# Attention probabilities split while still in PSUM, with half of each transpose moved to the DMA engines

## The chip, the cores and the metric

The kernel runs on one core of a Trainium2 chip. The metric is device time in microseconds (us) of one execution; lower is better. The core has five engines with programs of their own: TensorE (PE: matmuls and transposes, operands from SBUF, results to PSUM), VectorE (DVE), ScalarE (ACT), GpSimd (POOL, which here touches SBUF only) and SyncE (SP, which issues DMAs). Each runs its program strictly in order, and they meet at semaphores.

## The reference, cut to what matters

The input x is 4 sequences of 512 tokens of width 256, float32. It is layer-normalised, goes through attention, and independently through a mixture-of-experts layer; the output is x + attention * silu(experts).

```
xn = layernorm(x)
q, k, v = xn @ Wq, xn @ Wk, xn @ Wv          # 16 query heads, 4 key/value heads, head width 128
q, k = rotary embedding and positional scaling of q and k
scores = q k^T / sqrt(128), causal mask        # 512 x 512 for each of 4 x 16 heads
attn = softmax(scores)                         # exp(s - max) / sum
s = (attn @ v) @ Wo
g = silu(top-2-of-16 routed experts(xn) + shared experts(xn))
out = x + s * g
```

All matrix products are to be of nearly float32 precision. The kernel has no float32 matmul in its large products. It splits every operand into a 16-bit high half (float16) and a 16-bit low half (bfloat16, the rest after the high half is subtracted) and makes three passes: high*high, high*low, low*high.

## The kernel before, in words

The attention is done in 16 rounds (`NG`), one for each pair of batch and key/value head; a round has 4 query heads, 64 in all. Rounds 0, 1 and 2 ("first", "second", "third") also carry the transposes of the normalised x, the router and the placing of tokens with experts. Rounds 3 to 13 are a hardware loop over one body, round 14 runs the same body, and round 15 ("last") has no projections of queries and keys for a next round. Then come the expert steps: 40 tile steps of the shared experts and 48 tiles of the routed ones.

The order of the work on every engine is written out by hand in a `round_` function for each engine. All are built of stages j = 0, 1, 2 and a tail. Stage j works on the scores of head j+1 while the probabilities of head j are transposed; the tail transposes head 3 and scores the next round's head 0. Spread over the stages are the projections of the next round's queries and key (`project`, with their rotary products in `rotate_products` on DVE, a sum on POOL, the high half on ACT, the low half on POOL), this round's values (`project_values`), and the output projection of the last round's heads (`project_out`, added up by `add_projection` on DVE).

A head's probabilities go this way:

1. PE `score` (L1380): three passes of four causal row blocks of 128 queries with 128, 256, 384 and 512 keys, into three PSUM banks (units 0, 1, 2: the block of 512; the blocks of 384 and 128; the block of 256). A unit may be overwritten when its exponentials are done (L1386).
2. DVE `row_max` (L1089): adds the mask, takes the negated maximum of a row. Four instructions with four short reads of the accumulator.
3. ACT `exponentials` (L771): exp(s - max) from PSUM into `probs` in SBUF, float32, with the row sum as a by-product.
4. DVE `invert_sums` (L1100): one reciprocal of the four sums. It stands inside `rotate_products`, after the first of its three products.
5. POOL `divide` (L535): multiplies the probabilities by the reciprocal, four instructions.
6. PE `transpose_probs` (L1395): ten float32 transposes of 128x128 into two PSUM banks, in three units (4, 4 and 2 blocks). Units 0 and 1 stand early in the stage, unit 2 late.
7. ACT `probs_hi` (L781) copies each unit to SBUF as float16; DVE `probs_lo` (L1104) subtracts that from the bank and writes bfloat16. These are the halves of the transposed probabilities `pT`.
8. PE `weigh_values` (L1408): three passes of four matmuls over `pT` and the values, for head j-1 in stage j; ACT `output_hi` and DVE `output_lo` split the result.

SP issues its DMAs in the order of its own program: the weights, the fill of a DRAM buffer for routed rows, then (after the last attention weight is split) the shared experts' weights, and the routed experts' weights through a ring of five slots. `load_rows` (L478) later issues DMA transposes of 128x512 two-byte values from that DRAM buffer, once for each routed tile.

Of the kernel before, what the change touches and what calls it, by code (L numbers as in the profile page):

```python
# [10 lines left out]
F32 = mybir.dt.float32  # L11
# [7 lines left out]
P = 128  # L19
# [47 lines left out]
PCOLS = 1280  # L67

# [116 lines left out]
def build(nc, x, wq, wk, wv, wo, gate_t, w_gate_up, w_down, shared_gu, shared_down, rope, ident, mask, iota, tri, rows, digits, lag_digits, out):  # L185
    with ExitStack() as ctx:
# [74 lines left out]
        ARENA = 102400  # L261
# [20 lines left out]
        probs = [carve(PCOLS, F32) for _ in range(2)]  # L282
        pT = [split(PCOLS) for _ in range(2)]
# [32 lines left out]
        score_bank, pt_bank, o_bank, misc_bank = bank[0:3], bank[3:5], bank[5], bank[6:8]  # L316
# [17 lines left out]
        scores, maxed, exped, inverted, normed = sem("scores"), sem("maxed"), sem("exped"), sem("inverted"), sem("normed")  # L334
        pt_ps, pt_hi, pt_lo = sem("pt_ps"), sem("pt_hi"), sem("pt_lo")
# [21 lines left out]
        W_FIRST = 4  # L357

# [52 lines left out]
        def _(sp):  # L411
# [31 lines left out]
            sp.wait_ge(filled, 1)  # L443
            xs_tiles = xs_dram.rearrange("(t p) d -> p t d", p=P)
            for c in range(FILLS):
                sp.dma_start(xs_tiles[:, c * FILL_TILES:(c + 1) * FILL_TILES], fill).then_inc(fill_out, 16)

# [14 lines left out]
            for e in range(E_ROUTED):  # L462
                if e == ERING - E_SHARED:
                    sp.wait_ge(shared_w, 2)
                if e >= ERING:
                    sp.wait_ge(expert_low, e - ERING + 1)
                at = e % ERING * WE
                sp.dma_start(stage[:, at:at + WG].rearrange("p (c n) -> p c n", c=KC),
                             w_gate_up[e].rearrange("(c p) n -> p c n", p=P)).then_inc(expert_in[e % ERING], 16)
                sp.dma_start(stage[0:HC, at + WG:at + WE].rearrange("p (c n) -> p c n", c=2),  # L470
                             w_down[e].rearrange("(c p) n -> p c n", p=HC)).then_inc(expert_in[e % ERING], 16)
                if e == E_ROUTED - 1:

                    sp.wait_ge(scattered, SCATTERED)
                    sp.dma_start(meta[:], xs_tiles[:, :, D:DX]).then_inc(meta_in, 16)
# [247 lines left out]
        def _(act):  # L723
# [110 lines left out]
            def round_(rd):  # L834
                for j in range(GH - 1):
# [4 lines left out]
                    if j == 2:  # L840
                        output_hi(rd, 0)
# [783 lines left out]
```

## Time and profile before

| | us |
|---|---|
| median of 3 executions | 738.01 |
| lowest, highest | 737.32, 740.93 |
| span of the profiled execution, first to last instruction | 735.7 |
| PE busy (matmuls) | 659.1 |
| DVE busy | 581.6 |
| POOL busy | 537.8 |
| ACT busy | 442.3 |

No time of the profiled execution as a whole stands beside its span; the median lies 2.3 us above the span. In the profile "busy" is the time in which an engine has at least one instruction under way. Instructions of one engine overlap a little, so the distance between the starts of two successive ones is often shorter than the duration of the first; where an engine's capacity is the question, the distance between starts counts. A bracket at the end of a row gives the time that the engine stood idle before it and what it waited for. In names of tiles, "arena" is the large SBUF buffer in which most attention and expert tiles lie, and "bank" is PSUM.

The part of the page that follows the chain of work which ended last shows, by engine, shares of the span of 41% for POOL, 19% for issue, 17% for PE, 13% for DVE and 7% for ACT.

### The profile page before, as it was taken

What the parts mean: (1) busy time and instruction counts of PE and PEld (TensorE: products, weight loads), DVE (VectorE), ACT (ScalarE), POOL (GpSimd) and SP (SyncE); (2) the same over time, 40 slices, a digit from 0 to 9 for tenths busy, and PEclk for the clock granted to TensorE, in tenths of its full rate; (3) what the DMA queues carried; (4) which work ended last, traced back from release to release, by engine and by line L of the source; (5) the groups of instructions that cost most, each with busy time, mean ns of one, the idle gap of its engine ahead of it and who ended that gap; (6) DMA issues with size and microseconds to landing.
All of it is one profiled execution on the core that took longest, in us unless ns stands there. A gap on an engine that the chain in (4) does not pass through costs nothing.

```text
span 735.7 us, 17233 instructions
## 1 busy us (share of the span) xinstructions
PE 659.1 (90%) x4994; PEld 460.8 (63%) x4995; DVE 581.6 (79%) x1683; ACT 442.3 (60%) x1205; POOL 537.8 (73%) x588
## 2 busy tenths in 40 slices
PE   3678869789999999999999999999987899999992
PEld 1255546556766667676666766667665577767761
DVE  6988879789999999998999999999876344333378
ACT  3585636465657666575675657668584664555542
POOL 4677777978888887888877888888988993555510
PEclk9899989999999999999999999999998999999996
DMA  9491000500000000000000000000122564665772
GB/s 306 165 301 48 1 0 2 141 22 16 0 14 14 0 14 0 14 7 7 14 0 14 0 14 14 0 14 2 35 70 88 167 117 105 138 141 138 210 285 101
DMA packets 64952, 50.44 MB, mean 69 GB/s; under 512 B 35252, under 2 KB 58260, under 8 KB 64916
## 3 DMA queue, kind: packets, MB, share of 16 engines
q1 hardware_dynamic: 60804, 39.45, 19.3%
q0 software_dynamic: 3840, 10.52, 4.3%
q8 instruction: 20, 0.33, 0.2%
q14 instruction: 16, 0.13, 0.1%
q10 hardware_dynamic: 272, 0.02, 0.0%
HBM read 24.72 MB, written 18.96 MB: 59 GB/s over the span
## 4 chain that ended last, share of the span: by engine, by line
POOL 41%; issue 19%; PE 17%; DVE 13%; ACT 7%; DMA 2%; POOLq 0%; SPq 0%; DVEq 0%
POOL arena L539 16%; PE bank L1546 8%; POOL arena L533 8%; POOL arena L526 7%; PE bank L1576 6%; POOL xs_dram L586 4%; ACT arena L777 3%; POOL compare L582 2%; PE bank L1555 2%; DVE arena L1108 2%; POOL arena L563 1%; ACT arena L785 1%; DVE arena L1082 1%; DVE arena L1083 1%; DVE arena L1078 1%
## 5 line engine op out<-in xcount | busy, mean ns | idle before, releaser
L539 POOL TENSOR_TENSOR arena<-arena,rinv 128x128 f32<-128x128 f32 (+3 forms) x256 | 176.4, 720 | 83.5 <-DVE rinv L1102 83.4
L777 ACT ACTIVATE arena<-bank,nmax 128x512 f32<-128x512 f32 (+3 forms) x256 | 132.5, 535 | 64.6 <-DVE nmax L1096 64.6
L1096 DVE CUSTOM_DVE_ANT_0 bank<-bank,mask_b 128x512 f32<-128x512 f32 (+3 forms) x256 | 118.1, 516 | 14.2 <-issue 14.2
L1390 PE MATMUL bank<-arena 128*128 128x512 f16 (+7 forms) x768 | 116.4, 302 | 5.9 <-POOL arena L533 5.9
L785 ACT CAST arena<-bank 128x512 f16<-128x512 f32 (+1 forms) x192 | 93.3, 522 | 45.1 <-PE bank L1403 43.5
L1359 PE MATMUL bank<-xnT_hi,arena 128*128 (+1 forms) x320 | 111.0, 389 | 9.2 <-DVE arena L1083 4.7
L1419 PE MATMUL bank<-arena 128*128 128x512 f16 (+7 forms) x768 | 118.0, 305 | 0.0
L1403 PE MATMUL bank<-ident_f,arena 128*128 128x128 f32 x640 | 93.5, 277 | 25.5 <-DVE arena L1108 14.5
L1108 DVE TENSOR_TENSOR arena<-bank,arena 128x512 bf16<-128x512 f32 (+1 forms) x192 | 109.0, 595 | 3.9 <-ACT arena L785 1.8
L526 POOL TENSOR_TENSOR arena<-arena 128x512 f32<-128x512 f32 x77 | 98.6, 1281 | 2.5 <-DVE arena L1083 2.2
L1403 PEld LDWEIGHTS bank<-ident_f,arena 128*128 128x128 f32 x640 | 74.0, 142 | 38.9 <-DVE arena L1108 18.3
L1390 PEld LDWEIGHTS bank<-arena 128*128 128x128 f16 (+1 forms) x768 | 66.2, 98 | 48.1 <-issue 7.9
L533 POOL TENSOR_TENSOR arena<-arena 128x512 bf16<-128x512 f32 x80 | 92.5, 1161 | 4.8 <-ACT arena L765 4.8
L1435 PE MATMUL bank<-arena 128*128 (+2 forms) x768 | 94.6, 274 | 1.6 <-DVE logit L1048 1.2
L1419 PEld LDWEIGHTS bank<-arena 128*128 128x128 f16 (+1 forms) x768 | 68.3, 99 | 38.3 <-issue 2.4
L1435 PEld LDWEIGHTS bank<-arena 128*128 (+2 forms) x768 | 75.3, 98 | 19.9 <-issue 1.7
L1283 DVE TENSOR_TENSOR arena<-bank,arena 128x176 f32<-128x176 f32 x80 | 27.2, 340 | 73.3 <-ACT arena L912 71.8
L718 POOL DMA_INDIRECT ys_dram<-arena,row_u x48 | 46.0, 959 | 51.2 <-ACT arena L923 51.2
L765 ACT CAST arena<-arena 128x512 f16<-128x512 f32 x80 | 50.3, 629 | 53.9 <-POOL arena L526 49.3
L1359 PE MATMUL bank<-xnT_lo,arena 128*128 (+1 forms) x160 | 61.9, 387 | 0.0
L1359 PEld LDWEIGHTS bank<-xnT_hi,arena 128*128 (+1 forms) x320 | 31.9, 100 | 45.5 <-issue 8.3
L1082 DVE TENSOR_TENSOR arena<-bank,tab 64x512 f32<-64x512 f32 x80 | 55.4, 693 | 2.2
(147 smaller groups left out, 1158.9 us busy)
## 6 DMA issues: line engine op xcount, KB each, us to landing
xs_dram<-s_sb SPq DMA_DIRECT2D x4, 1548.0 KB, 14.4
stage<-w_gate_up SPq DMA_DIRECT2D x16, 352.0 KB
arena<-ys_dram SPq DMA_DIRECT2D x8, 512.0 KB, 6.5
stage<-w_down SPq DMA_DIRECT2D x16, 176.0 KB
stage<-wq SPq DMA_DIRECT2D x4, 512.0 KB, 8.0
stage<-wo SPq DMA_DIRECT2D x4, 512.0 KB, 6.5
stage<-x SPq DMA_DIRECT2D x1, 2048.0 KB, 10.6
out<-s_sb SPq DMA_DIRECT2D x8, 256.0 KB, 2.1
```

The lines of the kernel that those rows point to most:

```text
L526: pool.tensor_tensor(rot_a[buf], rot_a[buf], rot_b[buf], ALU.add).then_inc(rot_add, 1)
L533: pool.tensor_tensor(dst, rot_a[buf], hi, ALU.subtract).then_inc(rot_lo, 1)
L539: ins = pool.tensor_tensor(pr, pr, rinv[:, par, qt:qt + 1].to_broadcast([P, (qt + 1) * P]), ALU.mult)
L777: ins = act.activation(probs[par][:, P_AT[qt]:P_AT[qt] + n], score_bank[u][:, col:col + n], ACT.Exp, scale=-1.0, bias=nmax[:, par, qt:qt + ...
L785: act.copy(pT[j % 2][0][:, at:at + cols], pt_bank[(3 * j + u) % 2][:, 0:cols]).then_inc(pt_hi, 1)
L1096: ins = dve.tensor_tensor_reduce(score_bank[u][:, col:col + n], score_bank[u][:, col:col + n], mask_b[:, S - n:S], -1.0, 3e38, ALU.add, AL ...
L1108: dve.tensor_tensor(pT[j % 2][1][:, at:at + cols], pt_bank[(3 * j + u) % 2][:, 0:cols], pT[j % 2][0][:, at:at + cols], ALU.subtract).then_ ...
L1359: ins = pe.matmul(ps[:], w[a][:, c * chunk:c * chunk + DH], tokens[m][:, c * TOK:c * TOK + S], start=(c == 0 and n == 0), stop=(c == KC - ...
L1390: ins = pe.matmul(score_bank[u][:, col:col + n_k], qT[a][:, j * S + qt * P:j * S + (qt + 1) * P], kT[m][:, 0:n_k], start=(n == 0), stop=(n ...
L1403: ins = pe.transpose(pt_bank[(3 * j + u) % 2][:, col + (qt - kt) * P:col + (qt - kt + 1) * P], probs[j % 2][:, P_AT[qt] + kt * P:P_AT[qt] ...
L1419: ins = pe.matmul(o_bank[:, kt * P:S], v_s[a][:, kt * DH:(kt + 1) * DH], pT[j % 2][m][:, PT_AT[kt]:PT_AT[kt] + n_q], start=(kt == 0 and n ...
L1435: ins = pe.matmul(ps[:, 0:D], heads[a][:, j * S + q * P:j * S + (q + 1) * P], w[m][:, j * D:(j + 1) * D], start=(j == 0 and n == 0), stop= ...
```

## The change

- PSUM: the scores get four banks in place of three, used in turn (`score_at`: unit 3j+u modulo 4). The transposed probabilities get one bank, read as 2048 bytes of bfloat16 a partition, in place of two.
- ACT `exponentials` writes the exponentials back into the score bank in place.
- DVE `invert_sums` stands directly after `row_max`, and not within the rotary products.
- POOL `divide` is gone.
- ACT `probs_hi` now reads the exponentials in PSUM, multiplies by the reciprocal and writes the float16 high half `p_hi` of the untransposed probabilities: four instructions a head.
- DVE `probs_lo` now computes exponential * reciprocal - `p_hi` from PSUM in one instruction for a row block and writes bfloat16 `p_lo`: four instructions a head, the first block inside the rotary products, the other three behind them. A score bank is free when this is done, so PE `score` waits for `p_lo_ready`, where it waited for `exped`.
- SP `transpose_hi` transposes `p_hi` by four DMA transposes a head (of 4, 3, 1 and 2 blocks of 128x128), SBUF to SBUF, into `pT_hi`. SP's program gets the same rounds as the other engines; the loads of the experts' weights are placed between them.
- PE `transpose_probs` transposes `p_lo` only, ten bfloat16 transposes against a bfloat16 identity, in two units (8 and 2 blocks). ACT `pT_lo_out` copies them to SBUF.
- PE `weigh_values` makes the two passes over the high halves first (waiting for the DMAs), then the pass over the low halves.
- In stage 2, DVE's `output_lo` of head 0 stands between `row_max` and `invert_sums`, where it stood before `row_max`. In the tail, `output_lo` of head 2 stands before `row_max`, where it stood behind it; ACT's `probs_hi` for the next round's head 0 stands behind `rotate_hi("q2")` and the second `pT_lo_out`.

The core of the diff:

```diff
-PT_UNITS = [[(0, 0)], [(1, 0), (3, 384)], [(2, 0)]]
+PT_UNITS = [[(0, 0), (1, 512), (3, 896)], [(2, 0)]]
-PT_UNIT_COLS = [(0, 512), (512, 512), (1024, 256)]
+PT_UNIT_COLS = [(0, 1024), (1024, 256)]
+SCORE_BANKS = 4
...
-        probs = [carve(PCOLS, F32) for _ in range(2)]
-        pT = [split(PCOLS) for _ in range(2)]
+        p_hi = [carve(PCOLS, F16) for _ in range(2)]
+        p_lo = [carve(PCOLS, BF16) for _ in range(2)]
+        pT_hi = [carve(HI_COLS, F16) for _ in range(2)]
+        pT_lo = [carve(PCOLS, BF16) for _ in range(2)]
...
+            def transpose_hi(rd, j):
+                h, par = rd.head(j), j % 2
+                if not (isinstance(h, int) and h < 2):
+                    sp.wait_ge(pv, h - 1)
+                for u, unit in enumerate(SCORE_UNITS):
+                    sp.wait_ge(p_hi_ready, h * 3 + u + 1)
+                    sp.sem_inc(hi_seen)
+                    for qt, _ in unit:
...
+                        sp.dma_start_transpose(dst, p_hi[par][:, P_AT[qt]:P_AT[qt] + n].bitcast(BF16)).then_inc(pT_hi_in[par], 16)
...
-            def divide(h, par):
-                pool.wait_ge(inverted, h + 1)
-                for qt in range(QT):
...
                     for qt, col in SCORE_UNITS[u]:
+                        p = score_at(j, u)[:, col:col + (qt + 1) * P]
+                        ins = act.activation(p, p, ACT.Exp, scale=-1.0, bias=nmax[:, j % 2, qt:qt + 1], accum_out=rsum[:, j % 2, qt:qt + 1])
...
+            def probs_hi(rd, j):
+                h, par = rd.head(j), j % 2
+                act.wait_ge(inverted, h + 1)
+                if not (isinstance(h, int) and h < 2):
+                    act.wait_ge(pT_hi_in[par], hi_landed(rd, j - 2))
+                for u, unit in enumerate(SCORE_UNITS):
                     for qt, col in unit:
                         n = (qt + 1) * P
+                        ins = act.activation(p_hi[par][:, P_AT[qt]:P_AT[qt] + n], score_at(j, u)[:, col:col + n], ACT.Copy,
+                                             scale=rinv[:, par, qt:qt + 1])
+                    ins.then_inc(p_hi_ready, 1)
+
+            def pT_lo_out(h, j, units):
                 for u in units:
                     at, cols = PT_UNIT_COLS[u]
+                    act.wait_ge(pt_ps, h * 2 + u + 1)
+                    act.copy(pT_lo[j % 2][:, at:at + cols], pt_bank[:, 0:cols]).then_inc(pt_lo, 1)
...
                     if j == 2:
                         output_hi(rd, 0)
+                    exponentials(h, j + 1)
+                    pT_lo_out(rd.head(j), j, (0,))
+                    probs_hi(rd, j + 1)
...
                 dve.tensor_tensor(rot_a[buf], ps[:], tab[:, cos, :], ALU.mult)
                 half = DH // 2
-                if inverted_head is not None:
-                    invert_sums(*inverted_head)
+                if lows is not None:
+                    probs_lo(*lows, (0,))
...
             def probs_lo(h, j, units):
+                par = j % 2
                 for u in units:
+                    if u == 0 and not (isinstance(h, int) and h < 2):
+                        dve.wait_ge(pt_ps, h * 2 - 2)
+                    dve.wait_ge(p_hi_ready, h * 3 + u + 1)
+                    for qt, col in SCORE_UNITS[u]:
+                        n, at = (qt + 1) * P, P_AT[qt]
+                        ins = dve.scalar_tensor_tensor(p_lo[par][:, at:at + n], score_at(j, u)[:, col:col + n], rinv[:, par, qt:qt + 1],
+                                                       p_hi[par][:, at:at + n], ALU.mult, ALU.subtract)
+                    ins.then_inc(p_lo_ready, 1)
...
                 for j in range(GH - 1):
                     h, par = rd.head(j + 1), (j + 1) % 2
+                    row_max(h, j + 1)
                     if j == 2:
                         output_lo(rd, 0)
-                    row_max(h, par)
+                    if rd.first and j == 0:
+                        first_rope("q3", PROLOGUE.rot("q1"))
+                    invert_sums(h, par)
+                    if rd.first:
+                        x_items_lo(rd, X_BEFORE[j])
+                    rope(("q0", "q1", "k")[j], (h, j + 1))
...
-                probs_lo(rd.head(3), 3, (0, 1))
+                output_lo(rd, 2)
                 if not rd.last:
-                    row_max(rd.head(GH), 0)
-                output_lo(rd, 2)
+                    row_max(rd.head(GH), GH)
...
-                    if reuse:
-                        pe.wait_ge(exped, h * 3 + u - 2)
+                    if not (isinstance(h, int) and h * 3 + u < SCORE_BANKS):
+                        pe.wait_ge(p_lo_ready, h * 3 + u - (SCORE_BANKS - 1))
...
                     if u == 0:
-                        pe.wait_ge(normed, h + 1)
+                        pe.wait_ge(p_lo_ready, h * 3 + 3)
...
+                pe.wait_ge(pT_hi_in[j % 2], hi_landed(rd, j))
+                for a in range(2):
+                    for kt in range(QT):
+                        pe.matmul(o_bank[:, kt * P:S], v_s[a][:, kt * DH:(kt + 1) * DH], pT_hi[j % 2][:, hi_at(kt):hi_at(kt) + (QT - kt) * P],
+                                  start=(a == 0 and kt == 0), stop=False)
+                pe.wait_ge(pt_lo, h * 2 + 2)
+                for kt in range(QT):
+                    ins = pe.matmul(o_bank[:, kt * P:S], v_s[0][:, kt * DH:(kt + 1) * DH], pT_lo[j % 2][:, PT_AT[kt]:PT_AT[kt] + (QT - kt) * P],
+                                    start=False, stop=(kt == QT - 1))
```

## Rows read from the trace of the kernel before

**Rows 1.** Windows: length, busy PE, PEld, DVE, ACT, POOL; clock, DMA share, GB/s.

```profile
85.00:120.00 35.00, 27.67 (x190) 18.34 (x191) 27.06 (x80) 17.00 (x49) 23.71 (x28) 0.90 0.00 1
200.00:520.00 320.00, 314.99 (x2417) 219.98 (x2415) 294.85 (x856) 206.61 (x583) 264.27 (x296) 1.00 0.02 9
```

**Rows 2.** Waits, 200 to 520 us: who for whom; us, times, longest.

```profile
POOL arena L539 <- DVE rinv L1102: 50.4, 29, 3.1
...
DVE bank L1096 <- issue: 7.8, 10, 0.8
```

**Rows 3.** Page's costliest groups, POOL's divisions: busy us, mean ns; idle before.

```profile
L539 POOL TENSOR_TENSOR arena<-arena,rinv 128x128 f32<-128x128 f32 (+3 forms) x256 | 176.4, 720 | 83.5 <-DVE rinv L1102 83.4
```

**Rows 4.** Timeline of PE in the loop: start us, us, instructions.

```profile
302.46 1.47 PE L1435 MATMUL bank<-arena 128*128 x12
303.77 1.04 PE L1403 MATMUL bank<-ident_f,arena 128*128 128x128 f32 x8
304.65 1.79 PE L1419 MATMUL bank<-arena 128*128 128x512 f16 x12
306.60 1.80 PE L1390 MATMUL bank<-arena 128*128 128x512 f16 x12 [0.16 <-POOL arena L533]
308.24 0.38 PE L1359 MATMUL bank<-xnT_hi,arena 128*128 x1
308.45 0.38 PE L1359 MATMUL bank<-xnT_lo,arena 128*128 x1
...
317.50 0.28 PE L1374 MATMUL bank<-arena,xnT_hi 128*128 x2
```

**Rows 5.** Groups by form, 200 to 520 us: busy us, mean ns; idle.

```profile
L1108 DVE TENSOR_TENSOR arena<-bank,arena 128x512 bf16<-128x512 f32 x82 | 52.7, 684 | 1.3
...
L1108 DVE TENSOR_TENSOR arena<-bank,arena 128x256 bf16<-128x256 f32 x41 | 17.1, 417 | 0.3
...
L785 ACT CAST arena<-bank 128x512 f16<-128x512 f32 x82 | 44.0, 590 | 24.0 <-PE bank L1403 24.0
...
L777 ACT ACTIVATE arena<-bank,nmax 128x512 f32<-128x512 f32 x41 | 28.5, 695 | 34.6 <-DVE nmax L1096 34.6
```

**Rows 6.** Timeline of DVE: one head's row maxima and reciprocal.

```profile
312.84 0.69 DVE L1096 CUSTOM_DVE_ANT_0 bank<-bank,mask_b 128x512 f32<-128x512 f32 x1
...
314.61 0.14 DVE L1096 DVE_READ_ACCUMULATOR2_ANT nmax<- 128x1 f32 x1
...
315.90 0.18 DVE L1102 RECIPROCAL rinv<-rsum 128x4 f32<-128x4 f32 x1 [0.52 <-ACT arena L777]
```

**Rows 7.** Timeline of ACT: the same head's exponentials and casts behind.

```profile
313.63 0.69 ACT L777 ACTIVATE arena<-bank,nmax 128x512 f32<-128x512 f32 x1 [2.35 <-DVE nmax L1096]
...
315.75 1.08 ACT L785 CAST arena<-bank 128x512 f16<-128x512 f32 x2
316.70 0.65 ACT L765 CAST arena<-arena 128x512 f16<-128x512 f32 x1
```

**Rows 8.** Timeline of DVE: reciprocals around the early rounds, and the last one.

```profile
32.78 0.17 DVE L1102 RECIPROCAL rinv<-rsum 128x4 f32<-128x4 f32 x1
...
150.50 0.17 DVE L1102 RECIPROCAL rinv<-rsum 128x4 f32<-128x4 f32 x1
...
551.32 0.18 DVE L1102 RECIPROCAL rinv<-rsum 128x4 f32<-128x4 f32 x1 [1.25 <-ACT arena L777]
```

**Rows 9.** DMA transposes by source line; queue 1 from 600 to 680 us.

```profile
L480 SPq DMA_TRANSPOSE arena<-xs_dram x48: 1188/1193/4862, 593.6 to 689.1; - x48
...
DMA to landing us min/median/max: 2.6/3.3/4.8
...
q1 hardware_dynamic: 21927, 5.29, 36.4%
```

**Rows 10.** Timeline of PE in the last round.

```profile
555.36 0.66 PE L1403 MATMUL bank<-ident_f,arena 128*128 128x128 f32 x4 [2.33 <-POOL arena L539]
...
559.23 3.41 PE L1419 MATMUL bank<-arena 128*128 128x512 f16 x12
```

More of the change, by code:

```diff
@@ L459, in _ @@
             sp.dma_start(stage[0:SHARED_ROWS[-1], at + full * D:at + (full + 1) * D], shared_down[full * P:, :]).then_inc(shared_in, 16)
[L462 to L475, printed above, removed]
+            for e in range(ERING - E_SHARED):
+                load_expert(e)
+            with sp.Fori(3, NG - 2) as i:
+                round_(Round(i, "loop"))
+            round_(Round(NG - 2, "loop"))
+            sp.wait_ge(shared_w, 2)
+            for e in range(ERING - E_SHARED, ERING):
+                load_expert(e)
+            round_(Round(NG - 1, "last"))
+            for e in range(ERING + 1, E_ROUTED):
+                sp.wait_ge(expert_low, e - ERING + 1)
+                load_expert(e)
+            sp.wait_ge(scattered, SCATTERED)
+            sp.dma_start(meta[:], xs_tiles[:, :, D:DX]).then_inc(meta_in, 16)
             def load_rows(m, k):
@@ L808, in _ @@
             exponentials(0, 0, (1, 2))
+            probs_hi(Round(0, "first"), 0)
             normalise(1)
@@ L841, in round_ @@
                         output_hi(rd, 0)
+                    exponentials(h, j + 1)
+                    pT_lo_out(rd.head(j), j, (0,))
+                    probs_hi(rd, j + 1)
                     if j == 0:
-                        if rd.first:
-                            probs_hi(rd.head(j), j, (0, 1))
-                        exponentials(h, par)
-                        if not rd.first:
-                            probs_hi(rd.head(j), j, (0, 1))
                         rotate_hi("q3", rd.i * 5 + 5)
@@ L859, in round_ @@
                     else:
-                        probs_hi(rd.head(j), j, (0, 1))
-                        exponentials(h, par)
                         if rd.first:
@@ L881, in round_ @@
                     rotate_hi("k", rd.rot("k"))
-                probs_hi(rd.head(3), 3, (0, 1))
+                pT_lo_out(rd.head(3), 3, (0,))
                 output_hi(rd, 2)
@@ L887, in round_ @@
                 else:
-                    exponentials(rd.head(GH), 0)
+                    exponentials(rd.head(GH), GH)
                     rotate_hi("q2", rd.rot("q2"))
-                probs_hi(rd.head(3), 3, (2,))
+                pT_lo_out(rd.head(3), 3, (1,))
+                if not rd.last:
+                    probs_hi(rd, GH)
             round_(Round(0, "first"))
@@ L1193, in round_ @@
                             tile_experts(0)
-                    probs_lo(rd.head(j), j, (2,))
                     if rd.first:
@@ L1217, in round_ @@
                     tile_experts(1)
-                rope("q3", None if rd.last else (rd.head(GH), 0))
-                probs_lo(rd.head(3), 3, (2,))
+                if not rd.last:
+                    invert_sums(rd.head(GH), 0)
+                rope("q3", None if rd.last else (rd.head(GH), GH))
                 if rd.first:
```

150 lines of the change are left out of this document (78 added, 72 removed).

## The prediction

> **What bounds the kernel now.** I read the table of busy time by stretch first. From 200 to 520 us, nearly all of it the loop body, TensorE is busy 315.0 of 320 us and VectorE 294.9 [rows 1]. From 150.50 to 551.32 us lie 51 heads [rows 8], so a head takes 7.86 us and a round of four 31.4 us. TensorE is the bound; VectorE at 92% stands idle only 2.5 us a round. The waits say the same: the longest is GpSimd's wait for the reciprocal, 50.4 us, of an engine with time to spare, while VectorE's largest is 7.8 us in ten rounds, for scores [rows 2]. The page's chain gives GpSimd 41%, but each of its pieces is released by the other engines in turn, and TensorE is full; I do not read it as a GpSimd bound. The order of the steps then decides. The thing to see in the kernel before: the first rotary product, and in two stages of three also a head's two `probs_lo`, lie on VectorE between `row_max` and the reciprocal, so that the exponentials finish behind useful work.
>
> **TensorE.** The change halves the transposes. Eight float32 blocks take from 303.77 to 304.65, 0.11 us each; a 16-bit matmul of the same 128 columns adds about 0.06 (0.28 for two, of which one alone lasts some 0.22) [rows 4]. Ten a head: 0.55 us less, 2.2 us a round. The rest of TensorE's work is unchanged. Its need falls from 0.984 of 31.4 = 30.9 to 28.7 us a round.
>
> **GpSimd.** Four divisions go, 176.4 us in all, 2.75 a head [rows 3]. It is not the bound, so this pays only where others wait for it: in the early rounds.
>
> **ScalarE.** Out: casts of 1280 columns a head (590 ns for 512 [rows 5]; two in a row and the start of the next come 0.95 us apart [rows 7]), about 1.35 us. In: the same number of columns out of the bfloat16 bank, as one of 1024 and one of 256. No row shows a 1024-column cast from PSUM; twice the two casts' 0.475 is 0.95, and one instruction of that length saves one fixed part at most, so 0.85 to 0.95; I take 0.94. Also in: four scaled copies, no row; the exponentials, of the same shapes and with a pointer operand, are nearest (695 ns for 512 [rows 5]), the plain cast's 590 is the lower end. I take 0.69 us for the first and about 1.7 us of the engine for all. ScalarE's load goes from 206.6/320 of a round, 20.3 us, to about 26.5. It is no bound, but it stands in a chain.
>
> **VectorE.** Out: three subtractions, 684 + 684 + 417 ns [rows 5]. In: four instructions of 512, 384, 256 and 128 columns. By the slope between 684 and 417, 1.04 ns a column, they are 684 + 551 + 417 + 284 = 1936 ns, 0.15 us more a head, 0.6 a round. `scalar_tensor_tensor` is in no row; bounds -0.1 us a head (the four overlap at their edges) and +0.4 us (0.1 an instruction for the pointer operand, the excess of 695 over 590 on the other engine). Busy time a round: 0.921 x 31.4 = 28.9, plus 0.6 = 29.5 us. That is already above TensorE's 28.7: VectorE becomes the engine with the most work, and every wait in its program now lengthens the round. The new order makes three.
>
> *First wait: for the exponentials.* `invert_sums` stands right behind `row_max`. The last read of the maxima ends at 314.61 + 0.14 = 314.75; the exponentials end so that the reciprocal starts at 315.90 [rows 6], 1.15 us later, although they began at 313.63, right after the first maximum [rows 7]. In the last round the same wait shows at 1.25 us where nothing covers it [rows 8]. Before, the first product covered 0.6 of it or all. Now nothing does, but in stage 2 `output_lo` (about 0.6 us) lies in it. Per round 4 x 1.13 - 0.6 = 3.9 us.
>
> *Second wait: for the high half.* ScalarE, done with the exponentials, first copies 1024 transposed columns of the head before (0.94), then makes the high half of the first block (0.69), 1.63 us in all. VectorE meanwhile does the reciprocal (0.18) and the first product (0.69), and ScalarE's 1.63 began 0.1 before. 0.65 us remain a head, 2.7 a round (in the tail a rotary cast and a 256-column copy stand in place of the 1024-column copy, about as long). Bounds: 0.3 with the lower prices above, 1.1 if ScalarE is late for the transposes.
>
> *Third wait: in the tail.* `output_lo` of head 2 moved ahead of `row_max`. It needs, after VectorE's last low half but one: the bank that `add_projection` frees (0.8), `project_out` (1.31 us, 302.46 to 303.77), eight transposes (0.44), `weigh_values` (1.79) [rows 4], and `output_hi` on ScalarE (0.59, a cast like those of rows 5): 4.9 us. VectorE has 3.65 us of work there (0.35 + 0.35 + 0.6 + 2.0 + 0.35). 1.2 us a round; bounds 0 and 2.
>
> Sum of a loop round: 29.5 + 3.9 + 2.7 + 1.2 = 37.3 us, against 31.4: +5.9. Rounds 3 to 14 are twelve: +71. TensorE, 28.7 of 37.3 us, then has slack in each stage; the scores' new wait for `p_lo` costs it 0.3 us a head (the last unit), which falls into that slack.
>
> **Early rounds.** From the first reciprocal to the thirteenth the three take 117.7 us [rows 8]. From 85 to 120 us VectorE is busy only 27.1 of 35 [rows 1], partly waiting for the router's steps on GpSimd, which get 2.75 us a head of room. The same three waits would add 17.7; I give back 10: +8. **Last round and after.** No rotary products there; the end loses GpSimd's division between the last reciprocal and the last transposes (TensorE waits 2.33 us for it [rows 10]), gains ScalarE's and VectorE's steps: -2, bounds -4 and +3. The expert steps and their loads are unchanged. Total: +77.
>
> The profiled span is 735.7, the median 738.0, 2.3 above it. 735.7 + 77 + 2.3 = **815 us**.
>
> **DMA transposes.** Four DMAs a head go to SP's queue, 256 in all. In the expert steps a transpose of four blocks holds SP 1.19 us and lands 3.3 us after issue; queue 1 carried forty of them from 600 to 680 us at 36.4% of all engines, 0.73 us each [rows 9]. Ten blocks a head are 1.8 us of the DMA engines and at most 4.8 us of SP, inside 9.3 us. The high half is made about one and a half stages, 14 us, before `weigh_values` needs it, and the last of four issued in a row would land at about 8 us. So hidden; but these rows read DRAM, and none has SBUF as source. If the four run strictly one after another at 3.3 us, a head takes 13.2 us: a rival.
>
> **A rule that speaks for the change.** No row here has ScalarE writing to PSUM. The Trainium skill, "ScalarE: Activation LUTs", section on what happens when an `exp` ACTIVATE runs, says that ScalarE's writes to PSUM are faster than those to SBUF. By it the first wait would be shorter. No trace here can show it yet, and ScalarE still has to work off four instructions of which only the first overlaps the maxima, so it moves my sum by no more than the bounds below.
>
> **Rivals.**
> - *Only the first wait counts.* The scaled copies and the wide cast come out short, and the tail's chain is ready: 29.1 + 3.9 = 33.0 a round, +1.6 x 12 = 19, early +2, end -2: 757 us. For it: the two other waits are differences of small sums. Against: the 1024-column copy stands in the program between exponentials and high half, whatever its price. 14%.
> - *TensorE's clock falls in the gaps.* From 200 to 520 us it was granted in full (1.00, 2.4 GHz), from 85 to 120, with long gaps, 0.90 [rows 1]. After a gap of 2.33 us and another like it, twelve matmuls took 3.41 us in place of 1.79, its lower level of 1.2 GHz [rows 10, 4]. TensorE will now be idle 8 to 9 us a round, in pieces up to 2 us. At half clock the tail's chain is up to 3.5 us longer, and the score before each `row_max` 0.3 a head: +4.5 a round more, about 54: 869 us. The Trainium skill, "TensorE: Matmul & The Clock Gate", Part 1, says that activity releases the throttle and idle time brings it back; by that rule, which rows 10 agree with, this rival is live. Against it: between the gaps stand 5 to 7 us of dense work. 7%.
> - *Transposes from SBUF run one after another*, as above: ScalarE's `probs_hi` waits for the transposes two heads back and all follows: 64 x 13.2 = 845 in place of 519 (the 64 heads from 32.78 to 551.32): about 1060 us. 4%.
> - *Faster: TensorE stays the bound.* The mechanism: the exponentials, written to PSUM, end right behind the maxima, the high half follows at once, and TensorE keeps its order with 2.2 us less of transposes a round. It decides where VectorE's waits in sum fall below 31.4 - 29.5 = 1.9 us a round. Without any wait the round is 29.5, -1.9 x 12 = -23, early rounds -5, end -2: 708 us. Against it is the 1.15 us between the last maximum and the reciprocal, 3.9 a round, by itself too much. 6%.
> - *No change*, the same with waits of just that size: 2%.
>
> **How the numbers follow.** Forecast 67%, of its own 785 to 845 us; the rest as above. The range, 755 to 860, takes in the first rival and leaves out the clock's full price, the serial transposes and the faster side. Within 0.5% is about what a measurement of this kernel can tell from no change: 734 to 742. Slower 0.91, same 0.03, faster 0.06.
>
> **What would show it.** In the profile after: VectorE's idle time before `invert_sums` about 1.1 us a head, put down to ScalarE; idle before the first `probs_lo` about 0.65; idle before one `output_lo` a round about 1.2; a round of about 37 us; TensorE busy about 77% in the loop at a clock of 1.00; transposes on TensorE at half their spacing; DMA share near 0.2; no wait of TensorE or ScalarE on DMAs. It would be wrong if VectorE's low halves cost well below 0.5 us a block, if ScalarE's writes to PSUM shortened the exponentials by much, or if the DMA transposes held `weigh_values` up.

## The result and the profile after

The changed kernel takes 857.05 us (median of 4 runs, 856.83 to 857.18) where the kernel before takes 737.86: a ratio of 1.1605, interval 1.158 to 1.1631. Slower was forecast, and 857 lies inside the range of 755 to 860, 3 us below its upper end; the predicted 815 is 42 us too low.

The profiled execution took 857.14 us, its span 855.2. First the page of the kernel after: the busy times, the chain that ended last by engine, and three of its costliest groups (busy us, mean ns of one | idle of the engine before it, and for whom).

```profile
PE 659.4 (77%) x4930; PEld 428.3 (50%) x4995; DVE 605.0 (71%) x1747; ACT 544.7 (64%) x1397; POOL 365.2 (43%) x332
...
DVE 28%; PE 23%; ACT 21%; issue 20%; POOL 3%; DMA 2%; DVEq 1%; ACTq 1%; SPq 0%
...
L1167 DVE SCALAR_TENSOR_TENSOR arena<-bank,rinv,arena 128x512 bf16<-128x512 f32 (+3 forms) x256 | 128.8, 546 | 48.7 <-ACT arena L831 46.7
L839 ACT COPY arena<-bank 128x1024 bf16<-128x1024 bf16 (+1 forms) x128 | 91.9, 718 | 30.9 <-PE bank L1463 30.9
L1463 PE MATMUL bank<-ident_b,arena 128*128 128x128 bf16 x640 | 60.8, 229 | 54.1 <-ACT arena L839 54.0
```

No engine is full any more. The chain, 41% GpSimd before, is now shared about equally by VectorE, TensorE and ScalarE: work handed from one to the next and back. The next table is of the loop body of the kernel after, with the columns of [rows 1]:

```profile
250.00:600.00 350.00, 272.39 (x2059) 170.89 (x2092) 271.16 (x782) 235.29 (x616) 130.76 (x113) 0.97 0.17 40
```

TensorE is busy 78% of the stretch where it was 98% [rows 1], GpSimd 37%, and the DMA share is 0.17. The reciprocals of the heads mark the time, as in [rows 8]. In the kernel after it runs at 31.89 us (first head), 173.87 (thirteenth), 650.77 (61st) and 675.52 (last); before, at 32.78, 150.50, 531.44 and 551.32. So the 119.5 us of added span are:

- early rounds (three): 117.7 to 142.0 us, +24.3
- the twelve rounds between the thirteenth and the 61st: 31.75 to 39.74 us each, +96
- last round: 19.9 to 24.8 us, +4.9
- what lies ahead, -0.9; from the last reciprocal to the end (184.4 to 179.7), -4.7.

Where a round of another kernel is given below, it is the mean of the same twelve, read in the same way.

Where a loop round loses them is seen in the waits of the kernel after, 250 to 600 us (who for whom: us, times, longest), 8.8 rounds:

```profile
PE bank L1450 <- DVE arena L1167: 41.8, 34, 1.8
DVE rinv L1156 <- ACT bank L819: 36.9, 36, 1.2
DVE arena L1167 <- ACT arena L831: 25.8, 36, 1.4
PE bank L1463 <- ACT arena L839: 23.6, 18, 1.8
...
DVE arena L1174 <- ACT arena L853: 13.9, 9, 1.5
```

The three lines that begin with DVE are the three forecast waits, in the forecast places: 4.2, 2.9 and 1.6 us a round. With 30.8 us of work (271.16 of 350, of 39.74 us) they make 39.5 of the 39.74 us. TensorE's largest wait is for the low halves themselves, and its next for ScalarE's copy out of the transposes' bank: it follows VectorE and ScalarE. Its busy time, 30.9 us a round (272.39 of 350, of 39.74 us), is as large as VectorE's 30.8, so the busy times alone would not tell which of the two holds the round. Two stretches of VectorE's timeline show them at their instructions (the wait stands in brackets):

```profile
388.80 0.14 DVE L1150 DVE_READ_ACCUMULATOR2_ANT nmax<- 128x1 f32 x1
...
390.09 0.18 DVE L1156 RECIPROCAL rinv<-rsum 128x4 f32<-128x4 f32 x1 [1.16 <-ACT bank L819]
390.28 0.69 DVE L1131 TENSOR_TENSOR arena<-bank,tab 128x512 f32<-128x512 f32 x1
391.66 0.75 DVE L1167 SCALAR_TENSOR_TENSOR arena<-bank,rinv,arena 128x512 bf16<-128x512 f32 x1 [0.69 <-ACT arena L831]
...
408.41 0.69 DVE L1174 TENSOR_TENSOR arena<-bank,arena 128x512 f32 x1 [1.54 <-ACT arena L853]
```

What ScalarE did meanwhile, in its own timeline:

```profile
389.95 1.01 ACT L839 COPY arena<-bank 128x1024 bf16<-128x1024 bf16 x1
390.84 1.81 ACT L831 ACTIVATE arena<-bank,rinv 128x512 f16<-128x512 f32 x4
```

It copies the transposed columns of the head before first, and only then makes the high half that VectorE stands waiting for.

### The profile page after: what moved, and what is told of

Read it like the earlier page. It is cut to its first block, busy times and chain, and to the rows that moved or that the text cites. A ratio compares the mean times of both kernels' runs of the same rounds, so it can differ in the third digit from the quotient of the medians.

```text
span 855.2 us, 18017 instructions
## 1 busy us (share of the span) xinstructions
PE 659.4 (77%) x4930; PEld 428.3 (50%) x4995; DVE 605.0 (71%) x1747; ACT 544.7 (64%) x1397; POOL 365.2 (43%) x332
## 4 chain that ended last, share of the span: by engine, by line
DVE 28%; PE 23%; ACT 21%; issue 20%; POOL 3%; DMA 2%; DVEq 1%; ACTq 1%; SPq 0%
DVE arena L1167 11%; ACT bank L819 10%; PE bank L1608 7%; ACT arena L831 6%; PE bank L1638 5%; DVE arena L1136 3%; DVE arena L1135 3%; ACT arena L839 3%; PE bank L1497 2%; PE bank L1418 2%; PE bank L1477 2%; POOL arena L608 2%; DVE arena L1174 1%; PE bank L1617 1%; PE bank L1463 1%
## 5 line engine op out<-in xcount | busy, mean ns | idle before, releaser
L819 ACT ACTIVATE bank<-bank,nmax 128x512 f32<-128x512 f32 (+3 forms) x256 | 127.7, 500 | 142.3 <-DVE nmax L1150 142.3
L1450 PE MATMUL bank<-arena 128*128 128x384 f16 (+2 forms) x763 | 130.0, 307 | 75.4 <-DVE arena L1167 72.5
L1167 DVE SCALAR_TENSOR_TENSOR arena<-bank,rinv,arena 128x512 bf16<-128x512 f32 (+3 forms) x256 | 128.8, 546 | 48.7 <-ACT arena L831 46.7
L1450 PEld LDWEIGHTS bank<-arena 128*128 128x128 f16 (+1 forms) x768 | 64.3, 99 | 127.5 <-DVE arena L1167 91.1
L831 ACT ACTIVATE arena<-bank,rinv 128x512 f16<-128x512 f32 (+3 forms) x256 | 115.7, 556 | 0.5 <-DVE rinv L1156 0.5
L839 ACT COPY arena<-bank 128x1024 bf16<-128x1024 bf16 (+1 forms) x128 | 91.9, 718 | 30.9 <-PE bank L1463 30.9
L1463 PE MATMUL bank<-ident_b,arena 128*128 128x128 bf16 x640 | 60.8, 229 | 54.1 <-ACT arena L839 54.0
L1477 PE MATMUL bank<-arena 128*128 128x512 f16 (+3 forms) x512 | 88.1, 319 | 1.5 <-DVE arena L1174 1.5
L1463 PEld LDWEIGHTS bank<-ident_b,arena 128*128 128x128 bf16 x640 | 44.2, 103 | 79.7 <-ACT arena L839 62.2
L1477 PEld LDWEIGHTS bank<-arena 128*128 128x128 f16 (+1 forms) x512 | 47.3, 104 | 31.5 <-issue 7.1
L1174 DVE TENSOR_TENSOR arena<-bank,arena 128x512 f32 (+1 forms) x64 | 43.9, 685 | 26.8 <-ACT arena L853 26.7
```

What stands on the lines that cost most here:

```text
L819: ins = act.activation(p, p, ACT.Exp, scale=-1.0, bias=nmax[:, j % 2, qt:qt + 1], accum_out=rsum[:, j % 2, qt:qt + 1])
L831: ins = act.activation(p_hi[par][:, P_AT[qt]:P_AT[qt] + n], score_at(j, u)[:, col:col + n], ACT.Copy, scale=rinv[:, par, qt:qt + 1])
L839: act.copy(pT_lo[j % 2][:, at:at + cols], pt_bank[:, 0:cols]).then_inc(pt_lo, 1)
L1167: ins = dve.scalar_tensor_tensor(p_lo[par][:, at:at + n], score_at(j, u)[:, col:col + n], rinv[:, par, qt:qt + 1], p_hi[par][:, at:at + n] ...
L1450: ins = pe.matmul(score_at(j, u)[:, col:col + n_k], qT[a][:, j % GH * S + qt * P:j % GH * S + (qt + 1) * P], kT[m][:, 0:n_k], start=(n == ...
L1463: ins = pe.transpose(pt_bank[:, col + (qt - kt) * P:col + (qt - kt + 1) * P], p_lo[j % 2][:, P_AT[qt] + kt * P:P_AT[qt] + (kt + 1) * P], i ...
```

## The experiments

Twelve kernels: eight from the kernel after, four from the kernel before. Times are medians of the runs, ratios are to the kernel before (739.8 to 741.7 us in these batches).

### The order of two steps on ScalarE

```
                     exponentials(h, j + 1)
-                    pT_lo_out(rd.head(j), j, (0,))
                     probs_hi(rd, j + 1)
+                    pT_lo_out(rd.head(j), j, (0,))
```

> Changed kernel (857 us, loop round 40.2 us); in stages 0 to 2 ScalarE makes the high half of the new head before it copies the 1024 transposed low-half columns of the head before. Theory (VectorE is a chain of waits in program order): the second wait, 0.7 + 0.7 + 1.0 us a round before the first probs_lo, goes; 2.4 x 15 = 36 us, about 821 us, and the idle time before probs_lo is near zero in three stages. Rival (TensorE's one bank for transposes takes over): the copy is 1.8 us later, the second transposes and weigh_values behind it wait that much longer, the next scores come late and VectorE waits for them in place of the high half: 845 us or more.

Measured: 911.35 us, ratio 1.2292 (1.2214 to 1.2369); a round 43.96 us. Waits and stretch, 250 to 570 us:

```profile
PE bank L1463 <- ACT arena L839: 48.2, 20, 3.7
...
DVE bank L1150 <- issue: 24.7, 14, 3.1
...
250.00:570.00 320.00, 246.78 (x1706) 153.15 (x1734) 223.80 (x633) 192.51 (x494) 108.06 (x93) 0.88 0.15 36
```

The high half comes at once, and the copy comes late: both transposed units of a head share one bank, so TensorE waits for the copy (48.2 us in 7.3 rounds, against 23.6 in 8.8), the next scores come late, and VectorE waits for those instead. The rival (845 us or more) held, and the time went well beyond it. In this stretch TensorE's granted clock is 0.88 where it was 0.97; how much of the loss is the clock's and how much the late copy's is not separated. The second wait cannot be had back by turning these two steps round.

### The reciprocal and the low halves behind the rotary products

The reciprocal goes behind the first product and all low halves behind the whole rotary item, so that both waits have work in front of them (in round 0 the reciprocal stays where it was).

```
-                if lows is not None:
-                    probs_lo(*lows, (0,))
+                if lows is not None and inv:
+                    invert_sums(lows[0], lows[1] % 2)
...
-                        probs_lo(*lows, (1, 2))
+                        probs_lo(*lows, (0, 1, 2))
...
-                    invert_sums(h, par)
+                    if rd.first:
+                        invert_sums(h, par)
```

> Changed kernel; on VectorE the reciprocal stands again behind the first rotary product, and all three products stand before the head's low halves (in round 0 the reciprocal stays where it is). Theory: the exponentials are covered by 0.6 us of work and the high half by 1.4 us more: the first wait falls from 1.16 to 0.5 in three stages and to about 0 in one, the second to 0: 2.4 + 2.4 us a round, 15 rounds, about 785 us. Rival (TensorE or ScalarE sets the round, VectorE's waits are only where it shows): the waits move behind row_max or to output_lo, and the time stays above 840 us.

Measured: 784.68 us, ratio 1.0594 (1.0559 to 1.0629); a round 34.46 us. Timeline of VectorE, and the stretch 250 to 570 us:

```profile
409.76 0.18 DVE L1156 RECIPROCAL rinv<-rsum 128x4 f32<-128x4 f32 x1 [0.61 <-ACT bank L819]
...
411.39 1.93 DVE L1167 SCALAR_TENSOR_TENSOR arena<-bank,rinv,arena 128x512 bf16<-128x512 f32 x4
...
250.00:570.00 320.00, 276.72 (x2189) 178.74 (x2228) 282.00 (x830) 248.78 (x654) 145.24 (x124) 1.00 0.20 47
```

No instruction was added or taken away, and 72 us are back, as expected (about 785). The low halves start without a wait, the reciprocal waits less than half as long (17.4 us in 9.3 rounds against 36.9 in 8.8). VectorE is at 88% of the stretch; in the kernel before it was at 92% [rows 1].

### The DMA transposes left out

```
+                        continue
                         sp.dma_start_transpose(dst, p_hi[par]...)
...
-                pe.wait_ge(pT_hi_in[j % 2], hi_landed(rd, j))
```

> Changed kernel without the 256 DMA transposes and without the waits for them; weigh_values reads a high half that is zeroed once, so the attention output lacks its high part. Theory (the transposes are hidden): 857 us within 4 us. Rival (they hold up weigh_values, or their traffic slows the engines' SBUF accesses): 850 us or less.

Measured: 859.72 us, ratio 1.1617 (1.1583 to 1.1651), interval overlapping that of the kernel after. The DMA share falls from 0.17 to 0.02 (same columns as above) and nothing else moves:

```profile
250.00:600.00 350.00, 272.50 (x2065) 171.09 (x2099) 270.28 (x781) 233.95 (x613) 132.07 (x114) 0.97 0.02 7
```

The transposes from SBUF are hidden whole.

### The tail's order

```
-                output_lo(rd, 2)
                 if not rd.last:
                     row_max(rd.head(GH), GH)
+                output_lo(rd, 2)
```

> Changed kernel; in the tail VectorE's output_lo of head 2 stands behind row_max again, as in the kernel before. Theory A (the third wait, 1.5 us a round, is a wait for a chain that the scores need too, since score follows weigh_values on TensorE): VectorE then waits for the scores instead, and only the 0.6 us of output_lo that now lie in the wait for the exponentials are won: 0.6 x 15 = 9 us, about 848 us. Theory B (as my prediction put it, the wait is output_lo's own): 2.1 us a round, about 826 us.

Measured: 845.47 us, ratio 1.1432 (1.1401 to 1.1462); a round 38.77 us, 0.97 less. The wait of 1.54 us is gone, and VectorE waits ahead of the maxima instead, which leaves the reciprocal behind them a wait of 0.61:

```profile
402.93 0.69 DVE L1150 CUSTOM_DVE_ANT_0 bank<-bank,mask_b 128x512 f32<-128x512 f32 x1 [1.34 <-issue]
...
406.00 0.18 DVE L1156 RECIPROCAL rinv<-rsum 128x4 f32<-128x4 f32 x1 [0.61 <-ACT bank L819]
```

So the tail's wait costs 1 us a round net: its place is taken by the scores. This is theory A; theory B, the prediction's view that the wait is `output_lo`'s own, is out.

### TensorE kept busy in its gaps

```
+                    if warm and u > 0:
+                        for _ in range(8 - 2 * u):
+                            pe.matmul(o_bank[:], qT[0][:, 0:P], kT[0][:, 0:S], start=True, stop=True)
```

> Changed kernel; in stage 0 of each round but the first, TensorE runs 6 and 4 more matmuls of 512 columns into the bank that weigh_values overwrites next, in the two gaps (1.83 and 1.50 us) in which it waits for the low halves. Theory (the clock falls in these gaps, and the slower projection and transposes delay ScalarE's copy and with it VectorE's second wait in this stage, 1.0 to 1.4 us in place of 0.6): granted clock 1.00 in the loop, 0.4 to 0.8 us a round, 846 to 851 us. Rival (the clock costs nothing, all in slack): 857 us, or more by the added matmuls.

Measured: 858.34 us, ratio 1.1583 (1.1538 to 1.1628); a round 39.41 us.

```profile
250.00:570.00 320.00, 263.98 (x2011) 161.07 (x2009) 249.01 (x717) 215.71 (x566) 121.75 (x105) 1.00 0.17 39
...
DVE arena L1167 <- ACT arena L831: 21.2, 33, 0.7
```

The granted clock is back at 1.00. The second wait, by stage (tail, 0, 1, 2; means of the twelve rounds), goes from 0.57, 0.97, 0.69 and 0.69 us to 0.57, 0.65, 0.69 and 0.69: only that of stage 0, which has these gaps, gets shorter, and by as much as the round, 0.3 us. The added matmuls themselves delay nothing, for TensorE still waits for the low halves behind them:

```profile
412.38 0.83 PE L1455 MATMUL bank<-arena 128*128 128x384 f16 x6 [0.54 <-DVE arena L1167]
...
414.71 0.50 PE L1455 MATMUL bank<-arena 128*128 128x256 f16 x3 [0.64 <-DVE arena L1167]
```

So in the loop the fall of the clock to 0.97 costs 0.3 us of a round. The twelve rounds gain 4 us and the early ones 1, but from the 61st reciprocal to the end the profiled execution takes 3 us longer (204.5 to 207.7), and the time stays the same. The run adds nothing to round 0, where the granted clock is 0.83 with and without it.

### Reordering further

Three kernels on top of the reciprocal's move: with the reciprocal behind the second product and the tail order; with the reciprocal behind the first and the tail order; and with the low half's transposes in two banks, which takes one bank from the scores.

```
-SCORE_BANKS = 4
+SCORE_BANKS = 3
...
+        pt_bank = [b[:].bitcast(BF16) for b in bank[3:5]]
```

> Changed kernel with all rotary products before the head's low halves as in e2_cover (785 us, loop round 34.2 us), the reciprocal now behind the second product, and output_lo of head 2 behind row_max. Theory (VectorE's program-order waits are the loss): the remaining 0.61 us before the reciprocal goes in three stages, and 0.8 us a round in the tail as e4 measured: 2.6 x 15 = 39 us, about 746 us, VectorE busy 95% of the loop. Rival (with the waits gone, TensorE's single bank for transposes, for which it already waits 2.6 us a round, or ScalarE at 78% is next): not below 770 us.

> e2_cover with output_lo of head 2 behind row_max, the reciprocal where e2_cover has it, behind the first product. It tells which half of e9_cover_tail made that slower than e2_cover (791 against 785 us). If the later reciprocal did it (ScalarE waited up to 1.6 us for it where no 1024-column copy stands before the high half): 773 us, e2_cover less the 12 us that e4 gained. If the tail order did it (VectorE waited 1.06 us for the scores in place of output_lo): 785 us or more.

> e2_cover with three banks for scores and two for the transposed low halves, in place of four and one. Theory (the single bank costs little in the loop, where TensorE has slack, and some microseconds in the early rounds, where TensorE waited up to 4.1 us for ScalarE's copy): 775 to 783 us. Rival (the four score banks are needed now that a bank is held until the low half is done): 795 us or more.

Measured: 791.29 us (ratio 1.0669, 1.0631 to 1.0706), 786.59 us (1.0615, 1.0592 to 1.0639) and 791.8 us (1.068, 1.0657 to 1.0704); rounds of 34.90, 34.48 and 34.93 us. None beats 784.68. The second tells what made the first slow: the tail order alone gains nothing on top of the reciprocal's move (786.59), and the reciprocal behind the second product costs the other 4.7 us. In the first, ScalarE waits for the late reciprocal and VectorE for the late scores:

```profile
ACT arena L831 <- DVE rinv L1156: 16.2, 18, 1.6
...
407.21 0.69 DVE L1150 CUSTOM_DVE_ANT_0 bank<-bank,mask_b 128x512 f32<-128x512 f32 x1 [1.06 <-issue]
```

Its forecast of 746 missed by 45 us, its rival (not below 770) held: I had added the savings of two waits as if nothing stood behind them. The third was expected at 775 to 783 us, or at 795 and more if the four score banks are needed; it lies between. Its early rounds gain nothing (133.4 against 133.2 us), and TensorE's wait for low halves, which free the score banks, doubles from the 18.2 us of the kernel with the reciprocal's move alone to:

```profile
PE bank L1449 <- DVE arena L1167: 37.6, 19, 2.8
```

### The kernel before with only its reciprocal moved

```
             rotate_products(...):
-                if inverted_head is not None:
-                    invert_sums(*inverted_head)
...
                     row_max(h, par)
+                    invert_sums(h, par)
```

> Kernel before, one part of the change alone: the reciprocal stands directly behind row_max on VectorE in every stage. Theory (the order alone costs): VectorE waits 1.1 us a head for the exponentials with nothing beside it, 4.4 us a round, against 2.5 us of idle time that it had, of which part is used up: +2 to +4 us a round, 768 to 798 us. Rival (the order is harmless as long as TensorE is the bound, the loss comes from moving the split to PSUM): 738 to 745 us.

Measured: 806.74 us, ratio 1.0881 (1.0837 to 1.0925); a round 36.13 us, the early three 134.0. Waits and stretch from 250 to 570 us, then two reciprocals of round 0:

```profile
DVE rinv L1100 <- ACT arena L777: 51.3, 36, 1.8
...
250.00:570.00 320.00, 279.79 (x2109) 192.14 (x2107) 256.85 (x749) 179.91 (x505) 228.89 (x257) 1.00 0.02 8
...
43.55 0.18 DVE L1100 RECIPROCAL rinv<-rsum 128x4 f32<-128x4 f32 x1 [4.08 <-ACT arena L777]
55.37 0.18 DVE L1100 RECIPROCAL rinv<-rsum 128x4 f32<-128x4 f32 x1 [3.15 <-ACT arena L777]
```

One instruction a head, in another place, costs 65 us (806.74 against 741.69), more than half of what the whole change costs. VectorE's wait for the exponentials is 51.3 us in 8.9 rounds, 5.8 a round. I had forecast 768 to 798, with a wait of 4.4 us a round of which part falls into VectorE's idle time. The wait is longer (stages 1 and 2 have 1.8 and 1.6 us where I had 1.1): it grows by 5.3 us a round, and the round by 4.4, so little of it falls there.

### The kernel before without its parts' costs

No division on GpSimd (the `tensor_tensor` with `rinv` taken out, TensorE waits for the reciprocal in its place); 16-bit transposes (`probs` in bfloat16, as are the banks and the identity); and one half only (`probs` in float16, transposed once, no low half, its product pass left out).

```
-                    ins = pool.tensor_tensor(pr, pr, rinv[:, par, qt:qt + 1].to_broadcast(...), ALU.mult)
...
-        probs = [carve(PCOLS, F32) for _ in range(2)]
+        probs = [carve(PCOLS, BF16) for _ in range(2)]
...
-                    for n, (a, m) in enumerate(PASSES):
+                    for n, (a, m) in ((0, (0, 0)), (2, (1, 0))):
```

> Kernel before, one part of the change alone: GpSimd's divisions are left out, with nothing in their place, so the output is not normalised. Theory (they are off the path in the loop): the loop's 31.5 us a round stay, only the early rounds and the end gain, 725 to 736 us. Rival (the chain of waits is right that they carry 16% of the span): below 715 us.

> Kernel before with the probabilities kept in bfloat16 and transposed as such, so that its ten transposes a head take half the time; less exact output, all other steps as they were. Theory (TensorE is the bound at 98%, VectorE next at 92%): 2.2 us less of TensorE's work a round, of which VectorE's order lets 1 to 2 through: 712 to 725 us. Rival (the round is set by VectorE or GpSimd in the chain, TensorE is only full): 734 us or more.

> Kernel before with the probabilities kept and transposed as one float16 half; their low half, its subtraction on VectorE and its pass over the values are left out, so the output is less exact. It tells what the low halves cost in all and which engine is next. Theory: TensorE loses 4.4 us a round, VectorE 6.2, GpSimd at 26 us a round and TensorE at 26.6 bound the loop: 27.5 to 28.5 us a round, 685 to 700 us. Rival (the in-order chains give a smaller part, as in b3): 705 to 720 us.

Measured: 726.86 us (ratio 0.9805, 0.9777 to 0.9832), 730.17 us (0.9848, 0.9811 to 0.9886) and 719.21 us (0.9699, 0.9676 to 0.9723); rounds of 31.53, 31.11 and 30.33 us. Their stretches:

```profile
200.00:520.00 320.00, 312.95 (x2412) 220.64 (x2413) 292.96 (x849) 206.92 (x577) 157.86 (x135) 1.00 0.02 8
...
250.00:570.00 320.00, 294.42 (x2411) 196.96 (x2410) 264.18 (x819) 211.45 (x591) 273.04 (x303) 0.99 0.07 23
...
250.00:500.00 250.00, 224.34 (x1867) 149.84 (x1865) 193.53 (x609) 167.62 (x482) 217.82 (x246) 1.00 0.02 9
```

The two things that the change saves were worth 1.5 to 2%. Without the divisions the time is in the expected 725 to 736 us, and the rival is out: the chain of the page before puts 16% of the span on their line, and leaving them out gives 2%. The halved transposes give 0.64 us a round where I count 2.2 us less work on TensorE; 730 lies between the theory (712 to 725) and the rival. With one half only, the theory (685 to 700) is out and the rival (705 to 720) held. That third row shows no engine above 90% and a round only 1.4 us shorter; I read this as handovers that bound the round, as in the kernel after, but no run shows it.

## Why the prediction was right, and its 42 us

**The mechanism held.** VectorE became the engine on which the round hangs, in the three waits forecast, each larger than forecast, by at most 0.4 us a round. The hidden DMA transposes and the idle times of 1.16 and 0.69 us are as the prediction's last part asked; the round (39.7 us for 37), the tail's idle time (1.54 for 1.2) and the clock (0.97 for 1.00) are not. TensorE's 78% in the loop agrees with the 77% asked, but by luck: it is 30.9 us of 39.7 where I had 28.7 of 37.3, and even at a clock of 1.00, with the reciprocal moved, it is 29.8. The two experiments that move only the order bear the mechanism out from both sides: the reciprocal's place costs 65 us in the kernel before, and covering the first two waits gives back 72 of the kernel after. Of the third wait the cause was only half right: it is a chain that the scores need too, and moving `output_lo` back gives 1 us a round and not the 2.1 of theory B.

That 857 lies in the range owes something to the range's width: the loop is short by 25 us, the early rounds by 16. The 869 of the clock's rival lies nearer than my 815, but not for its reason, as the run with added matmuls shows.

**The sum of a loop round** was 29.5 + 3.9 + 2.7 + 1.2 = 37.3 us; measured it is 30.8 + 4.2 + 2.9 + 1.6 and 0.2 elsewhere, 39.7. The largest mis-sized term of it is VectorE's work, 1.3 us a round. The four `scalar_tensor_tensor` take, by form in the kernel after (xcount | busy us, mean ns | idle):

```profile
L1167 DVE SCALAR_TENSOR_TENSOR arena<-bank,rinv,arena 128x512 bf16<-128x512 f32 x36 | 27.0, 751 | 25.8 <-ACT arena L831 25.8
```

751 ns against the subtraction's 684 [rows 5]. All four sum to 2.18 us a head (546 x 4), where I took 1.94; of the bounds in the text, -0.1 and +0.4 us a head around 1.94, I took 0, and it is +0.25. In busy time the low halves went from 109.0 us in all to 128.8, 0.31 us a head in place of 0.15. That is 0.6 of the 1.3 us; 0.3 is the round itself, which I had taken as 31.4 from heads that include the shorter last round (the twelve take 31.75), and 0.4 I cannot place. The three waits add 0.9. Against the true 31.75 the rise is 8.0 a round in place of 5.9: 25 of the 42 us.

**Early rounds**: +24.3 in place of +8, 16 us of the miss. The step that failed is "I give back 10". GpSimd's freed time is worth little there: the kernel before with the division out gains 3.7 us in these rounds. Rounds 1 and 2 lose 5.5 and 6.6 us, nearly as much as a loop round. And in round 0 the reciprocal now stands ahead of the x items. Round 0 takes, before and after (the third row is the kernel before with only the reciprocal moved):

```profile
32.78:69.64 36.86, 28.07 (x238) 18.60 (x237) 33.00 (x89) 28.80 (x73) 27.65 (x29) 1.00 0.56 173
...
31.89:80.88 48.99, 34.33 (x256) 20.62 (x259) 34.86 (x96) 35.66 (x85) 16.34 (x13) 0.83 0.63 157
...
31.47:80.82 49.35, 35.02 (x242) 23.16 (x241) 35.68 (x94) 29.82 (x73) 27.21 (x29) 0.83 0.43 129
```

12 us in that round alone, and the one move by itself makes as much: VectorE waits up to 4.08 us for the exponentials, with the x items it could have made standing behind. TensorE's granted clock falls from 1.00 to 0.83 in both kernels shown with the move; what part of the 12 us that makes up no run separates. Early, the move by itself costs 16.3 us, of the 24.3 of the whole change.

**Last round and after**: +4.9 and -4.7 in place of -2 together, 1 us with what lies ahead.

**What stands between 785 and 738.** With two waits covered, a round is still 2.7 us longer than before. VectorE has 30.4 us of work a round there (282.00 of 320, of 34.46), 1.1 more than before (0.921 of 31.75), and still waits: 1.9 us for exponentials and 1.7 for the tail's output. I read the rest as these handovers; no experiment separates them further. Of the early rounds' remaining 15.5 us, 12.1 are round 0, where the reciprocal was left in front of the x items; no run moves it there too.

**The rivals.** "Only the first wait counts" (757) is out: the second and third are there. The clock did fall, as the second rival had it, but in the loop only by 0.03 and for 0.3 us of a round in place of 4.5. What the prediction held against that rival, 5 to 7 us of dense work between the gaps, was not so: between the two gaps shown below stand 0.83 us. In round 0 it fell to 0.83, and its price there stays open. The serial transposes are out, and so is "faster".

**Writes to PSUM, and the clock.** ScalarE's exponentials, now written to PSUM, are shorter, 662 ns for 512 columns where [rows 5] have 695:

```profile
L819 ACT ACTIVATE bank<-bank,nmax 128x512 f32<-128x512 f32 x36 | 23.8, 662 | 83.1 <-DVE nmax L1150 83.1
```

By the Trainium skill, "ScalarE: Activation LUTs", section "Step-by-step: what each stage is for", ScalarE writes faster to PSUM than to SBUF, and the trace agrees; but the wait behind the last maximum is 1.16 us where it was 1.15 [rows 6]. After TensorE's gaps a matmul of `project` takes 0.63 us where [rows 4] have 0.38, and the next starts 0.42 us behind it in place of 0.21: TensorE's lower level of 1.2 GHz.

```profile
414.34 0.83 PE L1450 MATMUL bank<-arena 128*128 128x384 f16 x6 [1.83 <-DVE arena L1167]
416.66 0.82 PE L1450 MATMUL bank<-arena 128*128 128x256 f16 x3 [1.50 <-DVE arena L1167]
417.28 0.63 PE L1418 MATMUL bank<-xnT_hi,arena 128*128 x1
417.70 0.63 PE L1418 MATMUL bank<-xnT_lo,arena 128*128 x1
```

The Trainium skill, "TensorE: Matmul & The Clock Gate", Part 1, says that idle time brings the throttle back. The trace agrees here too, and the run with added matmuls shows that in the loop this is 0.3 of the 8.0 us that a round loses.

## What to carry to other kernels

Before moving an instruction on an engine that works in program order, ask what it waits for and what useful work stands in front of it: here a reciprocal of 0.18 us, moved ahead of 0.7 us of independent work, cost 9% of the kernel. Taking work off an engine that is 98% busy was worth little here (0.64 of 2.2 us a round), with the next engine at 92%; that the handovers between the two are the reason is my reading. Savings of waits are not to be added up: behind each stood another (scores, a single bank, a late reciprocal).

## What the runs showed of the hardware

- `scalar_tensor_tensor` on VectorE with a PSUM source and a pointer scalar takes 751 ns for 128x512, 67 ns more than the subtraction it replaces.
- ScalarE copies 1024 bfloat16 columns out of PSUM in 1.01 us, more than the 0.94 I had taken from two 512-column casts.
- A DMA transpose from SBUF to SBUF, of 1 to 4 blocks, holds SyncE's queue 1.19 us at the median, as one from DRAM does [rows 9], so a head's four come to the 4.8 us that I had put. With what lies between them, first start to last end is 5.19 us in the head shown. They cost the kernel nothing. By source line, and in SyncE's timeline:

```profile
L474 SPq DMA_TRANSPOSE arena<-arena x256: 1177/1190/6331, 32.9 to 682.3; - x128
...
383.43 5.19 SPq L474 DMA_TRANSPOSE arena<-arena  x4
```

- TensorE's granted clock fell in the loop behind gaps of 1.83 and 1.50 us with 0.83 us of matmuls between them, and this cost 0.3 us a round; before, in the loop, it was 1.00 [rows 1].
